# A gated feed-forward layer with a conditioned adapter on one core: own buffers for tiles 1 to 3, new orders in steps 0 to 5 and in the last steps

## What is computed

```python
# x: 32 sequences x 256 positions x 256 channels; cond: 32 x 64
scale = cond @ norm_w.T + 1.0                       # per sequence, 256 channels
h = x * (scale[:, None, :] * rsqrt(mean(x*x, -1) + EPS))
val, gate = split(h @ up_w.T, 2)                    # 2 x 1024
h = val * gelu(gate)
h = round(h * 127/max|h|) / (127/max|h|)            # per position
w = clip(round(down_w / mean|down_w|), -1, 1) * mean|down_w|
x1 = h @ w.T + x
Wd_b = Wd + 0.1 * (cond @ Wdd.T + bdd)              # per sequence, 128 x 256
Wu_b = Wu + 0.1 * (cond @ Wdu.T + bdu)              # per sequence, 256 x 128
out = x1 + relu(x1 @ Wd_b.T + bd) @ Wu_b.T + bu
```

## Time and profile before

| | us |
|---|---|
| median of three runs | 479.8 |
| profiled execution, its own time | 480.11 |
| its span (first to last event on the core) | 478.4 |
| TensorE busy | 463.0 |
| VectorE busy | 374.0 |
| ScalarE busy | 365.0 |
| GpSimd busy | 258.7 |

### The profile page before, as it was taken

How to read it: one execution, slowest core, us unless ns; L and a number is a source line. 1 busy time by engine, 2 the same in 40 slices (tenths; PEclk the granted TensorE clock), 3 DMA queues, 4 the chain that set the end, 5 groups by cost and what they waited for, 6 DMA issues and landing times.

```text
span 478.4 us, 10014 instructions
## 1 busy us (share of the span) xinstructions
PE 463.0 (97%) x3266; PEld 267.1 (56%) x3266; DVE 374.0 (78%) x791; ACT 365.0 (76%) x636; POOL 258.7 (54%) x676
## 2 busy tenths in 40 slices
PE   6988899999999999999999999999999999999996
PEld 5434566555665545555555555555555555555564
DVE  2767888898988978877777877777788786778786
ACT  4586999999999877777768668676866867777664
POOL 0331756557565734655646375573746557344663
...
GB/s 286 372 51 60 152 263 181 226 182 209 259 180 227 83 83 131 131 136 125 134 127 117 132 151 125 140 133 120 116 141 154 110 155 125 81 138 133 79 76 111
DMA packets 118004, 70.99 MB, mean 148 GB/s; under 512 B 102017, under 2 KB 102977, under 8 KB 115905
## 3 DMA queue, kind: packets, MB, share of 16 engines
...
...
## 4 chain that ended last, share of the span: by engine, by line
PE 90%; DVE 4%; ACT 3%; issue 1%; DMA 1%; POOL 0%; ACTq 0%; DVEq 0%
PE bank L1125 63%; PE bank L1139 11%; PE bank L1200 5%; PE bank L1232 4%; PE bank L1218 4%; PE bank L1099 2%; DMA x<-in_norm_wT 1%; ACT hid L600 1%; ACT qn L609 1%; PE bank L1107 1%; ACT gel L587 1%; DVE hid L831 1%; PE bank L1072 0%; DVE adapt L777 0%; DVE xs_lo L810 0%
## 5 line engine op out<-in xcount | busy, mean ns | idle before, releaser
L831 DVE SCALAR_TENSOR_TENSOR hid<-bank,rms,gel 128x512 f32<-128x512 f32 x127 | 95.0, 749 | 83.1 <-ACT gel L587 79.7
L587 ACT ACTIVATE gel<-bank,rms 128x512 f32<-128x512 f32 x127 | 86.9, 685 | 93.1 <-PE bank L1125 87.4
L1125 PE MATMUL bank<-up_hi,xs_hi 128*128 128x512 f16 x492 | 146.5, 379 | 3.7 <-DVE hid L831 2.8
L1125 PE MATMUL bank<-up_hi,xs_lo 128*128 128x512 f16 x492 | 146.5, 379 | 0.2 <-DVE xs_lo L810 0.2
L1125 PE MATMUL bank<-up_lo,xs_hi 128*128 128x512 f16 x492 | 146.5, 379 | 0.0
L1125 PEld LDWEIGHTS bank<-up_hi,xs_lo 128*128 128x128 f16 x492 | 48.0, 98 | 58.6 <-DVE xs_lo L810 0.9
L1125 PEld LDWEIGHTS bank<-up_lo,xs_hi 128*128 128x128 f16 x492 | 48.0, 98 | 58.2
L839 DVE TENSOR_REDUCE amax<-hid 128x1 f32<-128x1024 f32 x63 | 76.8, 1219 | 2.1
L436 POOL TENSOR_TENSOR wsplit<-stage,wsplit 128x288 f16<-128x288 f32 x64 | 53.0, 857 | 45.1 <-ACT wsplit L561 45.1
L600 ACT ACTIVATE hid<-hid,amax 128x1024 f32<-128x1024 f32 x64 | 72.4, 1132 | 4.1 <-DVE amax L845 3.7
L1125 PEld LDWEIGHTS bank<-up_hi,xs_hi 128*128 128x128 f16 x492 | 46.7, 98 | 37.6 <-ACT gel L587 4.6
...
## 6 DMA issues: line engine op xcount, KB each, us to landing
...
qT<-qn SPq DMA_TRANSPOSE x63, 3.1
```

The lines of the kernel that those rows point to most:

```text
L587: nc.scalar.activation(gel[:, c], u_banks(t, c)[1][:], ACT.Gelu, scale=rms[:, t // TPB % XN_SLOTS, t % TPB:t % TPB + 1]).then_inc(gelu_don ...
L831: nc.vector.scalar_tensor_tensor(out=hid[:, t % 2, c * 512:(c + 1) * 512], in0=u_banks(t, c)[0][:], scalar=rms[:, t // TPB % XN_SLOTS, t % ...
L1125: ins = nc.tensor.matmul(dst[:], a[:, t // TPB % 2, k, cols], w[:, c, k, v, :], start=(k == 0 and n == 0), stop=(k == KD - 1 and n == 2))
```

## The change

Buffers: `gel` of tile 1 and `hid` of tiles 2 and 3 lie in a part of `adapt` that is generated later, and the waits on their predecessors fall away or name an earlier tile. `x1` has 22 tiles instead of 24. The start: eight and seven idle matmuls instead of six and four; the condition is the first load on SyncE's queue, the norm weights the first on ScalarE's, followed by x of sequence 0; the condition is scaled and split on GpSimd instead of VectorE. `up_first` works on one tile and one piece at a time. Orders of ScalarE's and VectorE's work in steps 0 to 4 are new, and the two sum matmuls go ahead of `up(3, 0)`. Generation begins one step later, so the adapters' steps begin at 24+(4b+2)/3. The last quantization: columns 0 to 383 on ScalarE and 384 to 1023 on VectorE; VectorE's pairs are transposed and taken up first. Both last output biases stand ahead of the low part of sequence 30. The stores of sequence 30 and of the last half are issued on ScalarE's queue. The diff, cut to its core and set eight columns to the left:

```diff
@@ -59,7 +59,7 @@
-X1_SLOTS = 24
+X1_SLOTS = 22
@@ -69,14 +69,15 @@
-IDLE_FIRST = 6
-IDLE_SECOND = 4
+IDLE_FIRST = 8
+IDLE_SECOND = 7
+ACT_COLS = 3 * P
@@ -86,7 +87,7 @@
-CHUNK_STEP = [FIRST + q for q in range(NGEN)]
+CHUNK_STEP = [FIRST + 1 + q for q in range(NGEN)]
@@ -171,6 +173,10 @@
+early = adapt[:, 1].rearrange("p b m -> p (b m)")[:, NC * 2048:]
+second_gel = early[:, 0:FF].rearrange("p (c f) -> p c f", c=NC)
+early_hid = [early[:, FF:2 * FF], early[:, 2 * FF:3 * FF]]
@@ -311,6 +318,12 @@
+def gel_of(t, c):
+    return second_gel[:, c] if t == 1 else gel[:, c]
+def hid_of(t):
+    return early_hid[t - 2] if t in (2, 3) else hid[:, t % 2]
@@ -374,15 +387,14 @@
-    def store_last():
-        for n, i in enumerate(LAST_ORDER):
-            sp.wait_ge(out_done, LAST_B + 1 + n)
-            sp.dma_start(out[LAST_B, :, i], late_out[:, i]).then_inc(stored_last, 16)
+    def store_last_first():
+        sp.wait_ge(out_done, B)
+        i = LAST_ORDER[0]
+        sp.dma_start(out[LAST_B, :, i], late_out[:, i]).then_inc(stored_last, 16)
+    sp.dma_start(cond2[0:C, :], condT).then_inc(ld_cond, 16)
     for n in range(NC * KD):
         sp.dma_start(raw_up[:, n // KD, n % KD], up_wT[:, n // KD, n % KD]).then_inc(ld_up[n], 16)
-        if n == 0:
-            sp.dma_start(xT_s[:, 0], xT[0]).then_inc(ld_xT[0], 16)
     sp.dma_start(xn_s[:, 0], xn[0]).then_inc(ld_xn[0], 16)
@@ -507,11 +519,31 @@
+    def split_cond():
+        pool.wait_ge(ld_cond, 16 * 2)
+        pool.wait_ge(ld_cond_again, 16)
+        nc.gpsimd.tensor_scalar(cond16[:], cond2[:], C_SCALE, None, ALU.mult).then_inc(cond16_ready, 1)
+        pool.wait_ge(const_ready, 4)
+        pool.wait_ge(cond16_ready, 1)
+        for half in range(2):
+            rows = slice(half * C, (half + 1) * C)
+            nc.gpsimd.tensor_scalar(cdiag_hi[rows, half], cond16[rows], 1.0, None, ALU.mult
+                                    ).then_inc(cdiag_ready, 1)
+        pool.wait_ge(cdiag_ready, 2)
+        for half in range(2):
+            rows = slice(half * C, (half + 1) * C)
+            nc.gpsimd.tensor_tensor(cdiag_lo[rows, half], cond16[rows], cdiag_hi[rows, half], ALU.subtract
+                                    ).then_inc(cdiag_ready, 1)
+        pool.wait_ge(cdiag_ready, 4)
+    split_cond()
@@ -544,8 +576,8 @@
     output_bias_last(1)
+    output_bias_last(0)
     middle_low(B - 2)
-    output_bias_last(0)
@@ -581,10 +613,12 @@
-        after(act, hid_done, (t - 1) * NC + c + 1)
+        held = 0 if t == 2 else t - 1
+        if t != 1:
+            after(act, hid_done, held * NC + c + 1)
-        nc.scalar.activation(gel[:, c], u_banks(t, c)[1][:], ACT.Gelu,
+        nc.scalar.activation(gel_of(t, c), u_banks(t, c)[1][:], ACT.Gelu,
@@ -596,7 +630,7 @@
-        part = hid[:, t % 2, 0:HALF] if t == LAST_T else hid[:, t % 2]
+        part = hid_of(t)[:, 0:ACT_COLS] if t == LAST_T else hid_of(t)
@@ -662,8 +696,8 @@
-    act.dma_start(cond2[0:C, :], condT).then_inc(ld_cond, 16)
     act.dma_start(normw, norm_wT).then_inc(ld_cond, 16)
+    act.dma_start(xT_s[:, 0], xT[0]).then_inc(ld_xT[0], 16)
     act.dma_start(cond2[C:2 * C, :], condT).then_inc(ld_cond_again, 16)
@@ -682,28 +716,30 @@
     scaled_high(1)
     squares(1)
     gelu(0, 0)
-    absolute_sum(0)
     gelu(0, 1)
     gelu(1, 0)
     gelu(1, 1)
-    squares(2)
+    absolute_sum(0)
+    absolute_sum(1)
     gelu(2, 0)
     quantize(0)
     quantized(0)
     gelu(2, 1)
-    absolute_sum(1)
     scaled_high(2)
+    squares(2)
     gelu(3, 0)
     quantize(1)
     quantized(1)
     gelu(3, 1)
     quantize(2)
     quantized(2)
-    squares(3)
     for s in range(FIRST, NT):
         for b in sequences(s, -1):
             relu(b)
         gelu(s, 0)
+        if s == FIRST:
+            gelu(s, 1)
+            squares(3)
         quantize(s - 1)
         if s < LAST_T:
             for t in split_tiles(s):
@@ -711,7 +747,7 @@
         quantized(s - 1)
-        if s < LAST_T:
+        if FIRST < s < LAST_T:
             gelu(s, 1)
@@ -733,6 +769,11 @@
+    act.wait_ge(out_done, B - 1)
+    act.dma_start(out[B - 2], out_s[:, (B - 2) % OUT_SLOTS]).then_inc(stored_last, 16)
+    act.wait_ge(out_done, B + 1)
+    act.dma_start(out[LAST_B, :, LAST_ORDER[1]], late_out[:, LAST_ORDER[1]]).then_inc(stored_last, 16)
@@ -825,18 +851,18 @@
         dve.wait_ge(gelu_done, t * NC + c + 1)
-        if c == 0:
-            after(dve, qn_done, t - 1)
+        if c == 0 and t >= 4:
+            after(dve, qn_done, t - 1 if t >= 6 else t - 3)
         nc.vector.scalar_tensor_tensor(
-            out=hid[:, t % 2, c * 512:(c + 1) * 512], in0=u_banks(t, c)[0][:],
-            scalar=rms[:, t // TPB % XN_SLOTS, t % TPB:t % TPB + 1], in1=gel[:, c],
+            out=hid_of(t)[:, c * 512:(c + 1) * 512], in0=u_banks(t, c)[0][:],
+            scalar=rms[:, t // TPB % XN_SLOTS, t % TPB:t % TPB + 1], in1=gel_of(t, c),
             op0=ALU.mult, op1=ALU.mult).then_inc(hid_done, 1)
         dve.wait_ge(hid_done, t * NC + NC)
-        nc.vector.tensor_reduce(a[:, 0:1], hid[:, t % 2], AX.X, ALU.max, apply_absolute_value=True
+        nc.vector.tensor_reduce(a[:, 0:1], hid_of(t), AX.X, ALU.max, apply_absolute_value=True
                                 ).then_inc(amax_done, 1)
@@ -882,12 +908,12 @@
-        nc.vector.tensor_scalar(hid[:, slot, HALF:], hid[:, slot, HALF:], a[:, 2:3], ROUND, ALU.mult, ALU.add
+        nc.vector.tensor_scalar(hid[:, slot, ACT_COLS:], hid[:, slot, ACT_COLS:], a[:, 2:3], ROUND, ALU.mult, ALU.add
-        nc.vector.tensor_scalar(qn[:, slot, HALF:], hid[:, slot, HALF:], ROUND, None, ALU.subtract
+        nc.vector.tensor_scalar(qn[:, slot, ACT_COLS:], hid[:, slot, ACT_COLS:], ROUND, None, ALU.subtract
@@ -1000,18 +1026,17 @@
     rsqrt_guess(1)
     gate(0, 0)
     gate(0, 1)
+    quant_scale(0)
     gate(1, 0)
-    quant_scale(0)
     gate(1, 1)
     gate(2, 0)
-    rsqrt_guess(2)
     quant_scale(1)
     gate(2, 1)
-    split_cond()
+    ternary_first()
+    gate(3, 0)
+    rsqrt_guess(2)
+    scaled_low(2)
     quant_scale(2)
-    gate(3, 0)
-    scaled_low(2)
-    ternary_first()
     gate(3, 1)
     ternary_second()
     ternary_third()
@@ -1083,30 +1108,27 @@
-            def up_first(c):
...
+    def up_first(t, c):
+        cols = slice(t * P, (t + 1) * P)
+        for k in range(KD):
+            if t == 0:
+                pe.wait_ge(up_hi_ready, c * KD + k + 1)
+            if t == 0 and c == 0:
+                pe.wait_ge(first_xs_hi, k + 1)
+            for n, a in enumerate((xs_hi, xs_lo)):
+                if t == 0 and c == 0 and k == 0 and n == 1:
+                    pe.wait_ge(xs_done, 1)
                 for v, dst in enumerate(u_banks(t, c)):
+                    nc.tensor.matmul(dst[:], a[:, 0, k, cols], up_hi[:, c, k, v, :],
+                                     start=(k == 0 and n == 0), stop=False)
+        for k in range(KD):
+            if t == 0:
+                pe.wait_ge(up_ready, c * KD + k + 1)
+            for v, dst in enumerate(u_banks(t, c)):
+                ins = nc.tensor.matmul(dst[:], xs_hi[:, 0, k, cols], up_lo[:, c, k, v, :],
+                                       start=False, stop=(k == KD - 1))
+        ins.then_inc(u_full, 1)
@@ -1157,10 +1179,10 @@
-        pe.wait_ge(qn_done, NT)
-        for n, pair in enumerate((0, 2, 1, 3)):
+        pe.wait_ge(last_qn_done, 1)
+        for n, pair in enumerate((2, 0, 3, 1)):
-                pe.wait_ge(last_qn_done, 1)
+                pe.wait_ge(qn_done, NT)
@@ -1169,12 +1191,13 @@
-        for n, (pair, arrived, count) in enumerate(((0, qT_a_done, 1), (2, qT_v_done, 1),
-                                                    (1, qT_a_done, 2), (3, qT_v_done, 2))):
+        order = ((2, qT_v_done, 1), (0, qT_a_done, 1), (3, qT_v_done, 2), (1, qT_a_done, 2))
+        for n, (pair, arrived, count) in enumerate(order):
-            for f in (2 * pair, 2 * pair + 1):
+            for j in range(2):
+                f = 2 * pair + j
-                                       start=(f == 0), stop=(f == JF - 1))
+                                       start=(n == 0 and j == 0), stop=(n == 3 and j == 1))
@@ -1263,15 +1286,17 @@
     for s in range(NT):
         if s < TPB:
-            up_first(s)
+            up_first(0, s)
+            up_first(1, s)
             continue
-        up(s, 0)
         if s == 3:
             pe.wait_ge(hid_done, NC + 1)
             pe.wait_ge(absum_ready, 2)
             nc.tensor.matmul(sum_ps, ones[:], wsum[:, 0:1], start=True, stop=False)
             nc.tensor.matmul(sum_ps, ones[:], wsum[:, 3:4], start=False, stop=True).then_inc(absum_full, 1)
+        up(s, 0)
         for t in downs(s, 0):
             down(t)
         if s < LAST_T:
```

53 lines of the change are left out of this document (10 added, 43 removed).

## The result

The changed kernel takes 473.6 us (median of four runs, 473.01 to 473.69), the kernel before beside it 479.47 (four runs, 478.88 to 479.81). The ratio is 0.9876, 95% interval 0.9859 to 0.9893: faster by 5.9 us, inside the range of the prediction, 2.3 above its forecast of 471.3. The profiled execution took 473.57 with a span of 471.8. All that follows reckons with spans: 478.4 - 471.8 = 6.6 us won. That is 0.7 more than the medians give, mainly because the profiled execution of the kernel before (480.11) lies 0.6 above the median of its runs.

A forecast was written before the change was run, and what follows sets the result against it. TensorE, busy 97% of the span, bounds the kernel, so only idle time and slow clock can be won. 8.1 us up to up(7,0) plus 0.4 in the tail gave 8.5: 471.6 from 480.11, forecast as a 471.3 median, range 469.3 to 474.6.

The forecast's parts named there:

- 1.0 of slow clock: Start: part of the 8.1 us gained up to up(7,0), from TensorE working less at the slow clock level.
- Norm weights: Start: landing forecast at 4 to 5 us, bounds 2.8 and 6.75; by the skill page alone only 0.58 won.
- The first rival: Start: norm weights land at 6.75, first product ends 13.5 to 14.1, some 2.3 us lost, 473.6; chance 0.15.
- The up weights are bytes on the same engines and land as before: Start: up weights' landing unchanged, so up_hi ends at 12.05 as before and up_lo at 13.3.
- VectorE's side ... done by 8.3: Start: VectorE's scaleT at 6.5, then xs_hi 0.6 and xs_lo 0.85, done by 8.3 against 10.25.
- Carrying one clock through the queues of steps 2 to 6: Steps 2 to 6: timing each queue by recorded distances put down(0) at 35.3, up(7,0) at 51.3; 5.6 us of stalls won.
- the second rival: Steps 2 to 6: a stall takes another's place; 0.5 us slips in five places add 2.5 to 3.5, 474.3; chance 0.13.
- down(2) is in time by 0.1: Steps 2 to 6: residual(1) ends at 42.0 and up(5,1) at 42.3, so down(2) does not stall.
- The single stall before down(3): Steps 2 to 6: TensorE waits 0.7 us, as residual(2) ends at 46.3 and up(6,0) at 45.7.
- The third rival: Middle: moved generation makes ScalarE's step longer than TensorE's in 16 steps; 8.8 us at 8.0 a step; chance 0.03.
- GpSimd's split of the condition: Start: five small instructions of 0.2 to 0.4 us each, ending before 11, costing nothing before sequence 1's root at 17.
- The tail: End of the kernel: transposes 0.2 us earlier and last store issued 0.2 earlier, together 0.4; bounds 0 and 0.8.

The follow-up runs named there:

- after: The changed kernel with the whole change, against the kernel before: 473.6 us, ratio 0.9876.
- the second execution of the start: Kernel before with only the start of the change, profiled once more to catch its slower group of runs: 480.54 us.
- the first experiment: Changed kernel with x of sequence 0 behind SyncE's first up weight, condition behind ScalarE's norm weights: 474.8 us; with two idle matmuls behind the scale product, 473.48.
- the last version: Changed kernel with sequence 2's root earlier, residual(2) ahead of tile 5's maximum, x of sequence 0 behind SyncE's first up weight: 471.75 us, ratio 0.9834.

## Why the prediction was right and wrong

**The bound and the sign** held: only idle time could be won, and 15.4 us of it became 7.5. The number held less well: of 8.5 us forecast 6.6 came in the traces and 5.9 at the median, and the range was wide because it took in the first two rivals. Of the time won, the buffers carry 3.5 (alone) or 3.0 (taken away from after), start 0.4 to 0.7 beside them, the tail 0.1. From start and buffers together (ratio 0.991) to after (0.9876) are some 1.6 us; what lies in them is the new orders of steps 0 to 4, the later generation and the tail, and these were not taken apart by a run. The two pauses of the middle (0.42 us of recorded idle time) belong to them: they stand in all five traces of versions that keep the old orders and the old step of generation (start, buffers, start and buffers, tail, and the second execution of the start), and in none of those that have the new ones. Which of the two removes them was not tried.

**The "1.0 of slow clock"** in the forecast's gain rests on one execution of the kernel before. In the trace of the buffers alone the same start had its four first products done 0.8 earlier, so a part of that gain is there in some executions without the change. The rise itself was put between 6.3 and 9; with the new idle matmuls it came between 4.7 and 10.9.

**Norm weights**, the step weighed longest: the forecast of 4 to 5 was on the cautious side, they land at 3.2 in after and at 4.4 in the latest of its kind. The DMA issues of the changed kernel in its first 60 us, to set beside the earlier trace rows:

```profile
x<-in_norm_wT ACTq DMA_DIRECT2D x1, 64.0 KB, 2.4
cond<-in_condT SPq DMA_DIRECT2D x1, 8.0 KB, 2.1
cond<-in_condT ACTq DMA_DIRECT2D x1, 8.0 KB, 7.7
```

In front of the bulk 64 KB land in 2.4 us, 5.9 before; the 8 KB behind x of sequence 0 take 7.7. Two places changed, their own and that of the bulk behind the condition, and the first experiment parts them: 5.3 to 5.9 with neither, 4.6 and 4.9 with the first alone, 2.0 to 3.6 with both. This agrees with the section "Issuing engines are not separate DMA queues" of the Trainium skill (DMA: Bandwidth & Descriptors) as far as it goes; that only the 0.58 of issue would be won, which I had read out of it, was wrong: 3.5 us more came from what no longer stood ahead. The first rival did not come. In the first experiment, where the condition is late instead, its first product ends 0.2 behind the rival's range, and its time lies 1.2 above after at the median; the rival was priced at 2.3 against a forecast that itself came 1.0 short.

**"The up weights are bytes on the same engines and land as before"** failed, and with it "VectorE's side ... done by 8.3". The chain that ended last, in order of time, in the changed kernel (start, length, what):

```profile
1.41 6.81 DMA xT_s<-in_xT
...
8.32 0.63 DVE xs_hi L787 x2
...
8.97 0.88 DVE xs_lo L836 x2
9.85 2.29 DVE up_lo L1020 x2
...
12.19 0.61 PE bank L1129 x2
```

Two things were not priced. x of sequence 0 moved to ScalarE's queue, behind the norm weights and at the same moment as the first up weight; it lands at 8.22, and VectorE waits 2.01 us for it. At its old place in the last version VectorE's wait ends at 7.77; it is 7.89 to 8.32 in the eight executions with the new place. And the condition's issue takes 0.58 us of SyncE's queue in front of all else:

```profile
0.79 0.58 SPq L395 DMA_DIRECT2D cond<-in_condT  x1
1.43 2.61 SPq L397 DMA_DIRECT2D adapt<-in_up_wT  x4
```

The up weights are issued from 1.43 on instead of 0.79, and the last up_hi starts at 12.03, 1.04 later than in the earlier trace rows. That is the latest of eight; the others with these loads have 11.59 to 11.95. Most of it is the condition's doing: with x back at its old place and the condition still first it starts at 11.55, with both back at 10.47 and 10.95. VectorE reaches up_lo at 9.77 and ends it at 14.43, forecast 13.3, before 14.78. TensorE has to wait for the second up_lo: 12.63 instead of 11.6. The prediction named both moves, priced the one DMA's landing and left the ones queued behind it at nothing: what a moved load does to those that stand behind it on its queue was not carried out. The slow clock cost little in this: with the same loads and the eight and seven idle matmuls the 2.4 GHz level came between 4.7 and 10.9 us in the profiled executions, and with six and four it was back at 11.8, yet the first product ended between 12.2 and 12.8 in all of them, since what it waits for last is x, its parts and up_lo.

**Carrying one clock through the queues of steps 2 to 6** was right for every engine but GpSimd. Its roots of sequence 2 stand nowhere in the sums of the prediction, so they were in effect taken to be in time. The twelve instructions of a root take 3.2 us in the trace of before (28.61 to 31.84); here they took 5.3. The last two of them in the changed kernel:

```profile
33.72 1.05 POOL L463 TENSOR_TENSOR nwt<-nwt,threehalf 128x2 f32<-128x2 f32 x1
34.85 1.18 POOL L470 TENSOR_TENSOR rms<-nwt 128x2 f32<-128x2 f32 x1
```

VectorE in the same stretch, and ScalarE behind it:

```profile
33.48 1.25 DVE L822 TENSOR_SCALAR x<-x 128x2048 f32<-128x2048 f32 x1
34.75 1.23 DVE L827 TENSOR_SCALAR tern<-x 128x2048 bf16<-128x2048 f32 x1
...
36.79 0.75 DVE L857 SCALAR_TENSOR_TENSOR hid<-bank,rms,gel 128x512 f32<-128x512 f32 x1 [0.81 <-ACT gel L621]
```

```profile
36.07 1.27 ACT L621 ACTIVATE gel<-bank,rms 128x512 f32<-128x512 f32 x2 [0.88 <-POOL rms L470]
```

Two instructions of two columns, 0.19 to 0.23 us each in the root of before, take 1.05 and 1.18, and each ends 0.04 to 0.05 us after the rounding of 2048 columns beside it (34.77 and 34.73, 36.03 and 35.98). ScalarE then waits 0.88 for the roots, VectorE 0.81 for the gelu, and TensorE stands 0.35 before up(5,0), and the stall before down(3) and short pauses before down(2) and the generated piece follow; with the 0.16 each as told they are 0.51, 0.29, 0.89 and 0.21. The gaps between down(0) and up(7,0) sum to 1.9 us where 0.75 were forecast: the missing 1.15. The experiment with the earlier roots gives 1.45 back, a part of it by VectorE's shorter list ahead of the maximum. So "a slip of 0.5 us in each of five places" (the second rival) was right in kind; it came in one place that neither it nor the forecast looked at, and it is why "down(2) is in time by 0.1" was no safe statement.

The trace of before had a row that shows the effect, which I did not read: GpSimd's three products of a single column at 35.79 take 1.49 us there beside VectorE's scaling of the down weights (35.94 to 37.23); in the changed kernel, with VectorE idle beside them, 0.47. The Trainium skill, SBUF — State Buffer, section "Who interferes with whom", has the rule: a tensor_scalar of VectorE in its two-port mode holds the port pair that GpSimd needs for the whole instruction. That these instructions run in that mode fits their length: 2048 columns in 1.25 us, where the maximum takes 1.21 for 1024. The ends 0.04 to 0.05 apart agree with it, and so does the instruction in front, which began at 33.45, before VectorE's at 33.48, and took its usual 0.20.

**The single stall before down(3)**: forecast 0.7, recorded 0.73, with the residual as releaser. That the sizes agree is in part luck: the stall came 2 us later than forecast, behind the late gelus, and in the version with the earlier root it is 0.36. **The third rival** is dead: no idle in the middle, ScalarE's 215.11 us of 280 as before. The 22 slots of x1 cost nothing. The 0.63 won in the middle was not forecast; it is the two pauses above.

**GpSimd's split of the condition** was forecast to end before 11. It begins when the second copy lands, at 10.15, and ends at about 14.9; the roots of sequence 1 come at 18.08, so the cover held, with 3 us left instead of 6. The five instructions were put at 0.2 to 0.4 us each and took 0.9 on average; whether that is their own length or VectorE's up_lo beside them was not tested.

**The tail.** The transposes start 1.55 after the last reciprocal, 1.73 before, so 0.18 of the forecast 0.2 came. The store is issued 0.30 nearer to it (10.43 against 10.73), where 0.2 was forecast. Between the two, 0.31 was lost on a cast of x1 that began 0.19 nearer to the reciprocal and ended 0.12 further from it. It lies in the same neighbourhood as above, this time with VectorE as the one that waits:

```profile
463.23 0.67 DVE L923 CAST x1n<-x 128x256 f16<-128x256 f32 x1
```

```profile
463.08 0.67 POOL L544 TENSOR_TENSOR wsplit<-stage,wsplit 128x256 f16<-128x256 f32 x1
```

This cast took 0.36 in before, where it met only the end of the same GpSimd instruction; in both kernels it ends 0.15 behind GpSimd's (470.24 and 470.09, now 463.90 and 463.75). The last output no longer waits 0.26 for its data, so these are again 0.13 nearer to the reciprocal than before, and the store stands 0.03 behind them instead of 0.20. The last store is then issued at 469.20 with its data ready at 469.17, and the span ends 0.14 earlier, not 0.30: the landing from the issue took 2.6 instead of 2.4. That difference is within the scatter of the tail: from the last reciprocal to the end two traces with the same code there differ by 0.36.
